# Expert attention on one core: two key groups kept on TensorE, masks on VectorE, a shared top-3 choice, a reordered last unit, semaphores cleared in ranges

## The reference

```
ss, sd = sigmoid(x @ Ws), sigmoid(x @ Wd)      # 8 heads x 5 experts per token, x normalised
ms, md = topk_mask(ss, 3), topk_mask(sd, 3)    # 1 for the three largest of five
q = sum_e (x @ Wq)[e]  * (sd * md)[e]          # 5 experts of 64 channels, for each head
k = sum_e (x @ Wk)[e]  * (ss * ms)[e]
v = sum_e (x @ Wv)[e]  * (ss * ms)[e]
out = softmax(q k^T / 8) v                     # 1024 keys, no mask
y = sum_heads sum_e md[e] * (out @ Wo[e])      # added to x
```

## Time and profile before

| what | before |
|---|---|
| median of 3 runs | 2741.61 us (2740.38 to 2743.81) |
| profiled execution, its own time | 2743.55 us |
| its span | 2741.8 us |
| PE / PEld | 2399.0 us (87%) / 1556.0 us (57%) |
| DVE | 1981.8 us (72%) |
| ACT | 1503.8 us (55%) |
| POOL | 1837.6 us (67%) |
| stages of expert attention, start to last addition | 1365.4 to 1983.0 and 2114.2 to 2732.6 us |

### The profile page before, as it was taken

How to read it: one execution, slowest core, us unless ns; L and a number is a source line. 1 busy time by engine, 2 the same in 40 slices (tenths; PEclk the granted TensorE clock), 3 DMA queues, 4 the chain that set the end, 5 groups by cost and what they waited for, 6 DMA issues and landing times. The chain is left out here.

```text
span 2741.8 us, 56038 instructions
## 1 busy us (share of the span) xinstructions
PE 2399.0 (87%) x21310; PEld 1556.0 (57%) x21310; DVE 1981.8 (72%) x3620; ACT 1503.8 (55%) x2069; POOL 1837.6 (67%) x1732
## 2 busy tenths in 40 slices
PE   6887787886899999999789999998788799999986
PEld 3555544644566676666556666665534466666655
DVE  7998545446677777777488888886286888888862
ACT  4222122322788888888625665556452256665564
POOL 1888100000999999999637899999610388999985
PEclk9899788988899999999889999999888999999998
DMA  1000000002689998899615555555411055555554
GB/s 44 1 1 0 0 23 13 1 23 64 123 159 161 151 157 162 150 153 163 118 49 90 96 93 95 95 95 97 76 31 53 20 99 94 93 93 93 95 102 80
DMA packets 763819, 226.74 MB, mean 83 GB/s; under 512 B 745992, under 2 KB 754696, under 8 KB 763552
## 3 DMA queue, kind: packets, MB, share of 16 engines
q1 hardware_dynamic: 763552, 223.16, 44.8%
HBM read 20.70 MB, written 1.05 MB: 8 GB/s over the span
## 5 line engine op out<-in xcount | busy, mean ns | idle before, releaser
L2275 PE MATMUL banks<-g_w,normed_t 128*128 128x320 f32 x1536 | 512.2, 460 | 42.2 <-DVE g_scratch L2580 38.3
L1575 POOL TENSOR_TENSOR g_p_lo<-g_p,g_p_hi 128x512 bf16<-128x512 f32 (+1 forms) x256 | 416.0, 1645 | 43.3 <-POOL g_z L2469 21.6
L1764 DVE TENSOR_REDUCE at_negmax<-banks 128x1 f32<-128x1024 f32 x256 | 301.5, 1219 | 154.6 <-PE banks L1676 154.6
L2275 PEld LDWEIGHTS banks<-g_w,normed_t 128*128 128x128 f32 x1536 | 265.7, 192 | 224.0 <-issue 81.0
L1741 POOL TENSOR_TENSOR at_p_lo<-at_p,at_p_hi 128x640 bf16<-128x640 f32 x256 | 356.0, 1407 | 13.2 <-ACT at_p_hi L1729 11.4
L1588 DVE TENSOR_REDUCE g_negmax<-banks 128x1 f32<-128x1024 f32 x256 | 310.3, 1217 | 32.8 <-PE banks L1499 30.4
L1565 ACT CAST g_r_hi<-banks 128x512 bf16<-128x512 f32 x128 | 74.9, 585 | 427.7 <-PE banks L1510 427.7
L1552 ACT ACTIVATE g_p<-banks,g_negmax 128x1024 f32<-128x1024 f32 x256 | 285.1, 1114 | 9.6 <-DVE g_negmax L1588 8.3
L1722 ACT ACTIVATE at_p<-banks,at_negmax 128x1024 f32<-128x1024 f32 x256 | 285.4, 1115 | 6.3 <-DVE at_negmax L1764 6.3
L1676 PE MATMUL banks<-at_k_t,at_q 64*128 64x512 f32 x1024 | 258.0, 623 | 18.5 <-POOL at_k_t L2025 9.7
L1499 PE MATMUL banks<-g_k_t,g_q 64*128 64x512 f32 x1024 | 254.4, 615 | 12.3 <-ACT g_p L1552 6.3
(11 more groups left out here) (414 smaller groups left out, 6327.3 us busy)
## 6 DMA issues: line engine op xcount, KB each, us to landing
at_swapped<-at_crossed SPq DMA_DIRECT2D x128, 128.0 KB, 2.8
g_w<-in_ex_w SPq DMA_DIRECT2D x2, 2880.0 KB, 11.5
f_w<-in_W SPq DMA_DIRECT2D x2, 1024.0 KB, 5.6
at_rope<-in_rope SPq DMA_DIRECT2D x1, 2048.0 KB, 9.8
at_t_hi<-at_p_hi SPq DMA_TRANSPOSE x128, 3.6
at_t_lo<-at_p_lo SPq DMA_TRANSPOSE x128, 3.6
g_t_hi<-g_p_hi SPq DMA_TRANSPOSE x128, 4.0
g_t_lo<-g_p_lo SPq DMA_TRANSPOSE x128, 3.8
```

The costliest lines, as they stand in the source:

```text
L1575: self.nc.gpsimd.tensor_tensor(self.part(self.p_lo, j, h), self.p[:, j % 2, h, 0:self.WIDTH[h]], self.part(self.p_hi, j, h), ALU.subtract) ...
L1764: self.nc.vector.tensor_reduce(self.negmax[:, j % 2, h:h + 1], self.core.banks[:, first:first + 2, :], AX.XY, ALU.max, negate=True).then_i ...
L2275: nc.tensor.matmul(out[:, 0:ED], core.xt[:, at:at + P], w[:, kind * H + tile // (T * BATCH) * 2 + h, :], start=True, stop=True).then_inc(p ...
```

## The change

- `KEPT` goes from 4 to 2: two blocks of head 0 stay on TensorE, p_hi and p_lo of head 0 grow from 512 to 768 columns, the transfers from 12 to 14 blocks.
- `dve_normalise` becomes `dve_route`. VectorE takes the reciprocal, multiplies the mask of 2 x 5 by it (`share`) and multiplies the sums in PSUM by that straight into `routed` (2 x 5 x 64). GpSimd's mask product goes, its additions stay. `dve_route` waits until GpSimd has added the step before the last.
- The choice is shared: VectorE compares by distance (four instructions a pair, bf16 results in `ahead`) and compares with 3 (`limit`); GpSimd counts (`count_duels`, eight instructions a pair) and multiplies the gates (`keep`). Only the first eight tiles of pair 0 are chosen whole on VectorE. Pairs 0 (rest) and 1 are counted before the steps, pairs 2 and 3 in steps 0 to 17.
- In the last unit the output projections stand later in TensorE's order, `add_out` later in VectorE's, and the first `place_out` earlier in ScalarE's.
- `clear` clears ranges of adjacent semaphore numbers.

```diff
     def clear(self):
-        for handle in self.in_use:
-            self.nc.gpsimd.sem_clear(handle)
+        numbers = sorted(handle.num for handle in self.in_use)
+        for first, last in self.runs(numbers):
+            self.nc.gpsimd.sem_clear(range(first, last + 1))
...
-    KEPT = CHUNK // P
+    KEPT = 2
...
-    WIDTH = (CHUNK, SEQ)
-    START = (0, CHUNK)
+    WIDTH = (SEQ - KEPT * P, SEQ)
+    START = (0, SEQ - KEPT * P)
...
-    def dve_normalise(self, dve, j):
+    def dve_route(self, dve, j, kept, added):
...
-        self.nc.vector.tensor_tensor(self.o[:, j // self.T % 2, j % self.T], o[:, :, 0:64], self.core.col(self.recip[:], 64),
-                                     ALU.mult).then_inc(self.o_ready, 1)
+        self.nc.vector.tensor_tensor(self.share[:], kept, self.core.col(self.recip[:], 5), ALU.mult).then_inc(self.share_ready, 1)
+        dve.wait_ge(self.share_ready, j + 1)
+        if j >= 2:
+            dve.wait_ge(added, j - 1)
+        self.nc.vector.tensor_tensor(self.routed[:, j % 2], o[:, :, 0:64].unsqueeze(2).to_broadcast([P, 2, 5, 64]),
+                                     self.share[:].unsqueeze(3).to_broadcast([P, 2, 5, 64]), ALU.mult).then_inc(self.o_ready, 1)
... TensorE, a step
-                if unit + 1 == UNITS and t > 2:
-                    project_out(*done_in(t - 1)[1])
                 beside(0)
                 hs.transpose(pe, j)
                 for k, tile in finishing[0:1]:
                     turn_out(k, tile)
+                if unit + 1 == UNITS and t > 2:
+                    project_out(*done_in(t - 1)[1])
...
-                for k, tile in finishing[0:1]:
-                    project_out(k, tile)
...
                 beside(2)
+                for k, tile in finishing[0:1]:
+                    project_out(k, tile)
+                for k, tile in finishing[1:2]:
+                    turn_out(k, tile)
... GpSimd
-                step(g.tensor_tensor(routed[:], hs.o[:, unit % BATCH, t].unsqueeze(2).to_broadcast([P, 2, E, D]),
-                                     mask[:, unit // BATCH, 1, 2 * tile:2 * tile + 2, :].unsqueeze(3).to_broadcast([P, 2, E, D]), ALU.mult))
...
+            for tile in range(T):
+                sum_queries(tile)
+            pool.wait_ge(counts_clear, 1)
+            for pair in range(2):
+                for k in range(8):
+                    count_duels(pair, k)
+            for pair in range(2):
+                keep(pair)
+            for tile in range(T, LEAD - 1):
                 sum_queries(tile)
             for j in range(STEPS):
                 for h in range(2):
                     hs.pool_lo(pool, j, h)
+                if j < 18 and j % 9 < 8:
+                    count_duels(2 + j // 9, j % 9)
+                elif j < 18:
+                    keep(2 + j // 9)
... VectorE
-            choose((0,), range(T))
+            choose_first()
+            dve.wait_ge(gates_ready, CHUNKS)
+            compare(0)
+            compare(1)
...
-            dve.wait_ge(gates_ready, CHUNKS)
-            choose((0,), range(T, 2 * T))
+            compare(2)
+            compare(3)
...
-                    choose((1,), range(2 * T))
...
-                for k, tile in finishing[0:1]:
-                    add_out(k, tile)
+                if unit + 1 == UNITS and t > 2:
+                    add_out(*done_in(t - 1)[1])
...
-                    hs.dve_normalise(dve, j - 1)
+                    route(j - 1)
                 beside(2)
...
-                for k, tile in finishing[1:2]:
+                for k, tile in finishing[0:1]:
                     add_out(k, tile)
-                if j < 30:
-                    choose_part(2 + j // 15, j % 15)
+                if j in (7, 16):
+                    limit(2 + j // 9)
```

More of the change, by code:

```diff
@@ L82, in clear, with runs @@
     def clear(self):
-        for handle in self.in_use:
-            self.nc.gpsimd.sem_clear(handle)
+        numbers = sorted(handle.num for handle in self.in_use)
+        for first, last in self.runs(numbers):
+            self.nc.gpsimd.sem_clear(range(first, last + 1))
         self.in_use = []
         self.nc.all_engine_barrier()
+    def runs(self, numbers):
+        starts = [n for n in numbers if n - 1 not in numbers]
+        return [(a, next(n for n in numbers if n >= a and n + 1 not in numbers)) for a in starts]
     def row(self, ap, tiles=TILES):
@@ L2216, in last_of, with rows_left, duels @@
             return 6 * T + 4 * (tile - T) + 2 * kind + 1 if tile < LEAD else first(tile - LEAD) + 2 * kind + 3
+        def rows_left(pair):
+            return slice(0 if pair else 2 * T, 2 * TILES)
+        def duels(d):
+            return slice((0, 4, 7, 9)[d - 1], (4, 7, 9, 10)[d - 1])
         def row_of(tile):
@@ L2459, in route @@
                 pool.wait_ge(hs.o_ready, j + 1)
[L2460 to L2464 removed]
+                one, two = (hs.routed[:, j % 2, h].rearrange("p e c -> p (e c)") for h in range(2))
                 if unit < BATCH:
@@ L2528, in limit, with choose_first @@
-            def limit(pairs, tiles):
-                count = part(mask, pairs, tiles)
-                step(v.tensor_scalar(count, count, float(TOP), None, ALU.is_lt))
-                dve.sem_inc(mask_ready, 1)
-            def keep(pairs, tiles):
-                own = part(gate, pairs, tiles)
-                step(v.tensor_tensor(own, own, part(mask, pairs, tiles), ALU.mult))
-            def choose(pairs, tiles):
+            def choose_first():
+                own, count, behind = (t[:, 0, :, 0:2 * T] for t in (gate, mask, lost.rearrange("p (z w n) e -> p z w n e", z=1, w=2)))
+                beat = [b.rearrange("p (w n) e -> p w n e", w=2) for b in beats]
@@ L2539, in choose @@
                 for e in range(E - 1):
-                    compare(pairs, tiles, e)
+                    step.later(v.tensor_tensor(beat[e], own[:, :, :, e:e + 1].to_broadcast([P, 2, 2 * T, E - 1 - e]), own[:, :, :, e + 1:E],
+                                               ALU.is_ge))
                 step.wait()
                 for e in range(E - 1):
-                    count_losses(pairs, tiles, e)
+                    step.later(v.tensor_reduce(behind[:, :, :, e], beat[e], AX.X, ALU.add))
@@ new lines, in choose_first @@
+                step(v.tensor_tensor(count[:, :, :, 0:E - 1], count[:, :, :, 0:E - 1], behind, ALU.subtract))
+                step(v.tensor_scalar(count, count, float(TOP), None, ALU.is_lt))
+                step(v.tensor_tensor(own, own, count, ALU.mult))
+            def compare(pair):
[3 more added lines that the diff above has]
+                ins.then_inc(compared, 1)
```

100 lines of the change are left out of this document (45 added, 55 removed).

## The result

The changed kernel's median is 2661.3 us (2656.08 to 2664.49, 4 runs), the kernel before's 2742.71 us (2740.38 to 2744.23, 4 runs): ratio 0.9702, 95% interval 0.9685 to 0.9720. The profiled execution took 2660.86 us, its span is 2659.0 us, 82.8 less than before.

| term | forecast | measured |
|---|---|---|
| *Clears* (gaps between stages and at the end, 34.3 to 12.6 us) | -22.5 | -21.6 |
| *Preparation* (start of the stage to first step, 76.4 and 74.6 to 67.7 and 67.8) | -3.5 | -15.5 |
| steps 0 to 55 (464.7 and 467.4 to 451.8 and 451.9) | -8 | -28.4 |
| *Last unit* (57.2 and 57.1 to 51.4 and 51.9) | -12 | -11.0 |
| *Tail* | 0 | -1.8 |

What follows compares the result with a forecast made beforehand. TensorE set the pace in unit 1 (7.76 us a step), GpSimd from unit 2 (8.33), VectorE nearly in step. Terms -22.5 - 3.5 - 8 - 12 = -46 us against the median of 2741.6 gave 2695 us, range 2672 to 2722.

Steps and rivals of the forecast that it cites:

- Clears: Gaps between stages: semaphores cleared in ranges, not one at a time, all on the path; -22.5 us, bounds -19 and -25.
- Preparation: Start of each expert stage, before its steps: the choice of the second pair leaves TensorE's idle time; -3.5 us for both stages.
- steps 0 to 55: Steps of both expert stages before the last unit: plain step 7.92 us; -8 us together, -26 at w = 0, +22 at w = 0.62.
- Last unit: Last seven steps of each expert stage, reordered: 7.3 us a step; -12 us for two stages, bounds -17 and -5.
- Tail: End of an expert stage: p_lo +0.5, transfer +0.3, routing 1.26 + 0.29 against 1.06; taken as 0.
- w: Wait of VectorE's share product for a running GpSimd instruction, fully added to VectorE's step of 7.67 us; 0.25 us, bounds 0 and 0.62.
- collisions: Preparation: VectorE's comparisons stretched while GpSimd counts duels in 16 short instructions; +1.7 us.
- Two kept groups: TensorE's work in a step: 0.07 us won, not 0.22, the second 0.10 nothing; plain step 7.70 us, turning steps 8.3.
- Masks on VectorE: Expert steps: GpSimd's step falls from 8.33 to 7.5 us, VectorE's becomes 7.67 + w, taken as 7.92.
- the coupling: Three projections of a step share one pair of spare banks, each waiting for the gating before: 2.26 us from gating to gating.
- the rival "w = 0": Expert steps: the share product slips between GpSimd's instructions without waiting; 18 us less, 2677 us; chance 0.27.
- The parts of the choice that left VectorE: Units 0 to 3 of an expert stage: these parts stood in VectorE's idle time, so removing them gives 0.

Runs made afterwards that it cites:

- the busy kernel: Kernel before plus unused matmuls on TensorE during the choice of pair 1, both expert stages: 18 gave 2744.29 us (ratio 1.0011), 12 gave 2736.61 us (0.9978).
- the old choice's run: Changed kernel with the whole choice of three back on VectorE, pairs 2 and 3 in steps 0 to 29: 2705.60 us, +44 against the changed kernel.

## Why the prediction was right in sign and wrong in size

Two steps of the prediction failed. One is the wait of the share product, taken as w = 0.25 us in every step; in most steps it is 0. The other is the preparation, taken as -3.5 us: its sum held collisions that came only in part, and put at nothing the lower granted clock behind TensorE's idle time.

*Clears*: right. 17 range clears stand in place of 329 single ones, and the gaps fell by 21.6 us. All of it is on the path; that more hangs on it is not shown.

*Preparation*: -15.5 us for -3.5. The forecast of 5.5 us for the choice of pair 1 held: TensorE's idle time before the 12 projections is 1.36 us, where it was 6.86.

```profile
1404.71 1.34 PE L2292 MATMUL banks<-g_w,normed_t 128*128 128x320 f32 x4 [0.84 <-DVE g_scratch L2589]
1407.42 3.60 PE L2292 MATMUL banks<-g_w,normed_t 128*128 128x320 f32 x12 [1.36 <-DVE g_scratch L2592]
```

What I set against it came only in part. Eight comparisons that ran while GpSimd counted took 3.62 us, where 3.2 and 1.7 for collisions were taken; the two comparisons with 3 before the steps took 0.18 and 0.23 us to the next start, where 0.5 was taken for each. And what I left out came: the row that I read, 5.33 us for 12 projections, showed the lower clock, which goes with the idle time. Without it they take 3.60, and the busy kernel shows that this is worth 1.8 and 2.2 us to the first scores. About 2 us more, at the start of the first expert stage, are not the change's: the busy kernels, which are the kernel before up to that point, reached their first turning of tokens 2.0 us sooner than it did. From 15 to 19 us into the stage the granted clock was 0.51 in the kernel before (1380.00 to 1384.00) and 1.00 in the busy one (1380.12 to 1384.12), by the same program. So of the 12 us the clock makes 4, the collisions and comparisons with 3 nearly 4, and chance 2; the other 2 were not taken apart.

*Two kept groups*: right. TensorE's steps came out as 7.71 and 8.32, forecast as 7.70 and 8.3, and of 0.32 us that TensorE loses only 0.06 is won. The step came where it was expected: from the scores to the second projection it is 4.26 us before and 4.18 after, for a forecast of 4.19.

*Masks on VectorE*: the form right, the size of w wrong, and it carries most of the 20 us of the steps. The forecast had VectorE's loop at 7.67 + w with the coupling in it; it is 7.57 with no wait, so that 0.14 us of a wait are free beside TensorE's 7.71. And w was not 0.25. For GpSimd's way from the end of a route to the end of p_lo I had 5.5 us "or a little more", with 0.76 for each addition to z; these take 0.86 and 0.94 to the next start (0.93 already in the kernel before, 2563.19 to 2564.12), the way is 2433.56 - 2427.68 = 5.88 us, and one sum of 0.81 later is the moment, 6.6 us by my own count, at which the share starts. The mean over 55 share products of the second stage is 0.237 us against 0.17 for one that meets nothing: w is 0.07, and in most steps 0: 41 of the stage's 64 took 0.17 to 0.18 us. A step of 7.71 us and not 7.92 in 80 plain steps is 17 us. This was the rival "w = 0" at 2677 us; together with the preparation it gives 2665.

```profile
L1604 DVE TENSOR_TENSOR g_share<-g_mask,g_recip 128x10 f32<-128x10 f32 x55 | 13.1, 237 | 1.9
```

The parts of the choice that left VectorE I had costed at nothing, since in the kernel before they stood in idle time. With the masks on VectorE that time is gone, and by the old choice's run they would have cost 18 us a stage: the cover of one edit was used up by another. The new choice isn't free in the steps either: two comparisons with 3 a stage stand behind p_lo and wait for it (1.52 and 1.53 us, at 2190.72 and 2266.41), and the steps that follow take 10.35 and 9.61 us where others of their kind take 9.04 and 8.17, 2.7 us a stage. The same shows in the sum of the parts: undone one at a time they cost 22, 85, 3, 44 and 17 us, 171 in all, for a change of 81.

*Last unit*: the order is worth what was forecast, but 11.0 us for 12 is in part luck. The steps are 6.56 us where nothing is late, not 7.3, which is TensorE's own work of the prediction (6.5); one or two of seven wait for a late transfer and then run at the lower clock, which the prediction did not have. Where the clock stays up, the last units take 47.05 and 47.49 us, 19.8 less than before; undoing the order cost 17.4 us by the medians.

The other stages' 4.6 us came from no edit that a run could show: linear attention and the stage behind it together took 200.2 us before and 197.1 after, and 197.0 to 199.9 in four other kernels that have the code of the changed one there.

## What to carry to other kernels

Where an instruction may wait for another engine's, count both engines' instructions with their start-to-start times from a common event and see which one is running at that moment; a mean over all of them is a poor stand-in, since the phase repeats from unit to unit. A duration read behind an idle stretch of TensorE carries the lower clock with it: price the work at the full clock if the change removes the idle time. The same holds for a wait that a change brings in: the step of 13.0 us is a late transfer and 9.4 us at the lower clock behind it. Where the same code differs by 4 us from stage to stage, as the last unit does, one trace of each kernel isn't enough to price an edit there. And price an edit that frees a cover and an edit that uses it together, in both orders.

## What the runs showed of the hardware

The share product, 10 elements with both inputs in SBUF, waits only for what is left of GpSimd's instruction beyond some 0.15 us: with 0.40 us left it took 0.42 us (2426.48), with 0.23 left 0.26 (2164.17), with 0.03 to 0.15 left 0.17 us, as alone. Where it was held up it ended 0.02 to 0.03 us after GpSimd's.

One input in SBUF is no safeguard either. The fourth of six tensor_scalars of 2 elements took 0.84 us, held by an addition to z (2434.27). The comparison with 3, a tensor_scalar of 320 elements, took 0.32 us at 1401.43, with nothing running on GpSimd until 1401.83, and 1.52 us at 2190.72, behind a p_lo:

```profile
1401.43 0.32 DVE L2575 TENSOR_SCALAR g_mask<-g_mask 128x320 f32<-128x320 f32 x1
...
2190.72 1.52 DVE L2575 TENSOR_SCALAR g_mask<-g_mask 128x320 f32<-128x320 f32 x1
...
2190.42 3.81 POOL L1582 TENSOR_TENSOR g_p_lo<-g_p,g_p_hi 128x768 bf16<-128x768 f32 x2 [0.24 <-POOL g_z L2479]
```

The Trainium skill (SBUF — State Buffer, "Who interferes with whom") names tensor_scalar among the instructions that can contend with GpSimd; by that rule the trace agrees. The prediction had taken only the rule on two inputs from there.

Added work can make a kernel faster: 24 unused matmuls, 12 in each of two stages, took 6 us off the kernel before (3.6 to 8.5).
